# Output projection in seven block products over two query groups, and the first statistics spread by TensorE

## The chip, the cores and the metric

The kernel runs on one core of one Trainium2 chip. Its engines are TensorE (PE, matmuls into PSUM), VectorE (DVE), ScalarE (ACT), GpSimd (POOL) and SyncE (SP, which here only issues DMAs). The metric is the device time of one execution in microseconds; a profiled execution also gives the span from the first to the last event of the program.

## The reference

Input x is [2, 2048, 2048], so T = 4096 tokens of C = 2048 features; D = 512.

```
xn   = layernorm(x)                                # no scale, no shift
qkv  = xn @ Wqkv + bqkv ; q, k, v = split(qkv)     # Wqkv [2048, 1536]
attn = softmax(q @ k.T / sqrt(512)) @ v            # per batch of 2048 tokens
a    = attn @ Wo + bo                              # Wo [512, 2048]
s    = (xn @ Wq.T) @ keys.T                        # router, 64 experts
gate = softmax over the 16 largest of s, 0 elsewhere
z    = (xn @ A.T) * gate, each gate over 8 columns # A [512, 2048]
out  = x + a + 2 * (z @ B.T)                       # B.T [512, 2048]
```

## The kernel before, in words

All matmuls are made in three passes: each operand is split into a high part (a copy into the 32-bit type of TensorE, on ACT) and a low part (what is left, on DVE), and high x high, high x low and low x high are added up in one PSUM bank. Hence the names `w_hi`/`w_lo`, `r_hi`/`r_lo`, `q_hi`/`q_lo`, `p_hi`/`p_lo`, `f_hi`/`f_lo`.

**Phase A** (`phase_a`, 0 to about 1376 us) makes k, q, z and v for four groups of 1024 tokens. In each group the product of the normalised x with the weights is done as seven block products (`ORDER`, idx 0 to 6) of eight steps (s), in which two half-sized blocks of x and of the weights, or sums of them, meet. Mean and reciprocal deviation of a token are statistics over its row; they are needed as rows over all partitions (`mean_rstd`). For the first 512 tokens TensorE spreads them (a product of ones with a diagonal, L775). For the second 512 tokens of the first group, ACT (`moments`) and DVE (`stats_of_tile`) compute them in idx 0, ACT stores them to `stat_scratch` (L549) and loads them back broadcast (L555), and `normalise` of DVE waits for that (semaphore `s_mld`), in idx 1, ahead of its own next `split_weights`.

**Phase B** (`phase_b`) goes through eight query groups t of 512 queries. Its matmuls come in items: an item is one [128, 1024] block of keys, values or weights, held in a ring of four slots (`r_hi`, `r_lo`), and takes 24 matmuls. A turn is `scores(t)` (8 items), `output(t-1)` (16 items, the projection of the previous group: 8 column-and-input pieces of z and of attention per column block of 512), `values(t)` (8 items). The softmax of group t (maximum over the keys, `query_maxima`, spread of the maximum by TensorE, `less_maximum` on DVE, `exponential` on ACT, `sums` on POOL) runs beside `output(t-1)`; group 0 has no output to run beside, so `softmax_start` stands between `scores(0)` and `values(0)`. The low parts of the probabilities (`p_lo`) are made in `values`, from a ring of four.

The first time that a block is used it is split on the chip and stored to `split_scratch` (`keep`); later it is loaded in both parts (`fetch`). SP runs through its own program and waits at each load for the slot, four items ahead. The order of each engine's work is that of the Python functions of the same name: each engine works through its program in order, and a wait holds up all behind it.

In `output`, the residual rows of x are loaded into `res`, POOL adds the bias to them (L1770), DVE adds the finished PSUM bank (`take_output`, L1877), and SP stores the tile, 256 KB at a time. The attention result is taken in `take_attention` and split into `f_hi`/`f_lo`; z is transposed by TensorE.

## Time and profile before

| | |
|---|---|
| median of 3 runs | 2846.6 us (2846.41 to 2846.97) |
| profiled execution, time | 2843.56 us |
| profiled execution, span | 2841.0 us |
| PE busy | 97% of the span |
| DVE / ACT / POOL busy | 53% / 30% / 14% |
| HBM traffic | 223 GB/s over the span |

The first row is what a comparison of two kernels goes by. The profiled execution is a single one; its span is what the positions in the trace add up to. "Busy" is the time in which an engine has an instruction shown; on PE such instructions overlap each other.

### The profile page before, as it was taken

The numbers are of one execution on the slowest core, as the hardware profiler recorded it, in microseconds if no ns is written. First come the engines' busy times: TensorE is split into PE (matmuls) and PEld (weight loads), VectorE is DVE, ScalarE is ACT, GpSimd is POOL, SyncE is SP. The second block draws the span as 40 slices with busy tenths as digits, with TensorE's granted clock in tenths as the row PEclk, the third lists the DMA queues.
The fourth block names the chain that finished last, engine by engine and source line by source line (L and its number), as shares of the span: only waits on it lengthen the run. The fifth ranks groups of instructions, "written<-read, shape, count | busy, mean of one in ns | idle before, by whom it ended". The sixth has DMA issues, their size and how long they took to land.

```text
span 2841.0 us, 33300 instructions
## 1 busy us (share of the span) xinstructions
PE 2749.1 (97%) x12096; PEld 2244.6 (79%) x12096; DVE 1496.1 (53%) x1875; ACT 854.7 (30%) x1146; POOL 389.6 (14%) x293
## 2 busy tenths in 40 slices
PE   6888999999999999999979999999999999999999
PEld 4676878878888888888868788888888888888887
DVE  6665876467745776455574634324444344333431
ACT  3552225622364233322242221111322212112110
POOL 0011000000000000000031504205032050320501
PEclk9999999999999999999989999999999999999999
DMA  7589665455555364324766967758688686775866
GB/s 299 184 300 319 218 209 199 148 163 178 174 200 157 119 216 138 97 97 163 253 244 247 343 226 253 279 203 296 240 275 303 238 287 216 250 281 197 284 233 234
DMA packets 268159, 636.01 MB, mean 224 GB/s; under 512 B 30192, under 2 KB 54896, under 8 KB 263792
## 3 DMA queue, kind: packets, MB, share of 16 engines
q1 hardware_dynamic: 233968, 546.54, 56.2%
q10 hardware_dynamic: 28288, 66.62, 6.8%
q0 software_dynamic: 5760, 20.97, 2.1%
q8 instruction: 86, 1.41, 0.2%
q14 instruction: 57, 0.47, 0.1%
HBM read 499.79 MB, written 134.25 MB: 223 GB/s over the span
## 4 chain that ended last, share of the span: by engine, by line
PE 85%; DVE 5%; DMA 4%; ACT 3%; issue 2%; SPq 0%; POOL 0%; ACTq 0%; DVEq 0%; POOLq 0%
PE psum L750 35%; PE psum L1632 15%; PE psum L1634 15%; PE psum L1633 15%; PE psum L687 2%; DMA stat_scratch<-mv 2%; DMA w_raw<-t_scratch 1%; ACT rows L534 1%; DVE prob L1834 1%; DMA w_raw<-W_blocks 1%; DVE r_lo L1806 1%; ACT w_hi L479 1%; DVE w_lo L800 1%; ACT rows L537 1%; PE psum L1755 0%
## 5 line engine op out<-in xcount | busy, mean ns | idle before, releaser
L800 DVE TENSOR_TENSOR w_lo<-w_raw,w_hi 128x1024 fp32r<-128x1024 f32 x224 | 274.2, 1224 | 433.7 <-ACT w_hi L479 433.5
L479 ACT ACTIVATE w_hi<-w_raw 128x1024 fp32r<-128x1024 f32 x224 | 237.5, 1060 | 775.2 <-PE psum L750 677.8
L1632 PE MATMUL psum<-r_hi,f_hi 128*128 128x512 f32 x1024 | 401.9, 392 | 4.6 <-DVE r_lo L1806 3.3
L1634 PE MATMUL psum<-r_hi,f_lo 128*128 128x512 f32 x1024 | 399.2, 390 | 0.0
L1633 PE MATMUL psum<-r_lo,f_hi 128*128 128x512 f32 x1024 | 399.1, 390 | 0.0
L750 PE MATMUL psum<-s_hi,w_hi 128*128 128x512 f32 x896 | 353.7, 395 | 28.1 <-DVE w_lo L800 16.4
L750 PE MATMUL psum<-w_hi,s_hi 128*128 128x512 f32 x896 | 351.4, 392 | 15.9 <-DVE w_lo L800 14.9
L750 PE MATMUL psum<-s_hi,w_lo 128*128 128x512 f32 x896 | 351.3, 392 | 0.0
L750 PE MATMUL psum<-s_lo,w_hi 128*128 128x512 f32 x896 | 351.3, 392 | 0.0
L750 PE MATMUL psum<-w_lo,s_hi 128*128 128x512 f32 x896 | 350.3, 391 | 0.0
L750 PE MATMUL psum<-w_hi,s_lo 128*128 128x512 f32 x896 | 350.2, 391 | 0.0
L1770 POOL TENSOR_TENSOR res<-res,b_out 128x512 f32<-128x512 f32 x128 | 183.5, 1463 | 798.3 <-DMA res<-x 798.2
L1877 DVE TENSOR_TENSOR res<-psum,res 128x512 f32<-128x512 f32 x128 | 86.9, 691 | 366.5 <-PE psum L1634 347.5
L1632 PEld LDWEIGHTS psum<-r_hi,f_hi 128*128 128x128 f32 x1024 | 192.5, 188 | 48.7 <-DVE r_lo L1806 4.6
L750 PEld LDWEIGHTS psum<-s_hi,w_hi 128*128 128x128 f32 x896 | 169.7, 189 | 69.7 <-DVE w_lo L800 16.5
L1634 PEld LDWEIGHTS psum<-r_hi,f_lo 128*128 128x128 f32 x1024 | 192.6, 188 | 40.5
L1633 PEld LDWEIGHTS psum<-r_lo,f_hi 128*128 128x128 f32 x1024 | 192.7, 188 | 39.2
L1632 PE MATMUL psum<-p_hi,r_hi 128*128 128x512 f32 x512 | 206.8, 404 | 11.4 <-DVE p_lo L1926 6.7
L750 PEld LDWEIGHTS psum<-w_hi,s_hi 128*128 128x128 f32 x896 | 169.0, 189 | 56.4 <-DVE w_lo L800 16.2
L1632 PE MATMUL psum<-q_hi,r_hi 128*128 128x512 f32 x512 | 200.0, 391 | 2.5 <-DVE r_lo L1806 1.7
L1634 PE MATMUL psum<-p_hi,r_lo 128*128 128x512 f32 x512 | 201.5, 394 | 0.0
L1633 PE MATMUL psum<-p_lo,r_hi 128*128 128x512 f32 x512 | 201.2, 393 | 0.0
(137 smaller groups left out, 3931.5 us busy)
## 6 DMA issues: line engine op xcount, KB each, us to landing
r_hi<-split_scratch SPq DMA_DIRECT2D x208, 512.0 KB, 3.5
r_lo<-split_scratch SPq DMA_DIRECT2D x208, 512.0 KB, 4.9
w_raw<-t_scratch SPq DMA_DIRECT2D x128, 512.0 KB, 4.0
w_raw<-W_blocks SPq DMA_DIRECT2D x96, 512.0 KB, 3.9
res<-x SPq DMA_DIRECT2D x128, 256.0 KB, 6.1
out<-res SPq DMA_DIRECT2D x128, 256.0 KB, 7.2
rows<-x ACTq DMA_DIRECT2D x29, 1024.0 KB, 5.8
xb<-xT ACTq DMA_DIRECT2D x56, 512.0 KB, 6.1
```

Source lines behind the costliest of these rows:

```text
L479: nc.scalar.activation(w_hi[:, s % RAW], w_raw[:, s % RAW], ACT.Copy).then_inc(s_whi, 1)
L534: chain.link(nc.scalar.activation(tile, tile, ACT.Identity, accum_out=total[:, col]))
L537: chain.link(nc.scalar.activation(tile, tile, ACT.Square, bias=less_mean[:, col], accum_out=squares[:, col]))
L687: mm = pe.matmul(psum[0:M_R, bank, :], wq[:, block_k + k, :], t[:, k, :], start=(k == 0 and n == 0), stop=(k == HK - 1 and n == 1))
L750: mm = pe.matmul(psum[:, bank, :], stationary, moving, start=(k == 0 and n == 0 and not chained), stop=(k == HK - 1 and n == 2), skip_grou ...
L800: nc.vector.tensor_tensor(w_lo[:, s % RAW], w_raw[:, s % RAW], w_hi[:, s % RAW].bitcast(F32), ALU.subtract).then_inc(s_wlo, 1)
L1632: pe.matmul(bank, sh, mh, start=first, stop=False)
L1633: pe.matmul(bank, sh, ml, start=False, stop=False)
L1634: return pe.matmul(bank, sl, mh, start=False, stop=last)
L1770: nc.gpsimd.tensor_tensor(res[:, slot, :], res[:, slot, :], b_out[:, c * W:(c + 1) * W], ALU.add).then_inc(b_xb, 1)
L1806: nc.vector.tensor_tensor(r_lo[:, slot, :], r_raw[:, slot, :], r_hi[:, slot, :].bitcast(F32), ALU.subtract).then_inc(b_lo, 1)
L1877: nc.vector.tensor_tensor(res[:, tile % XO, :], psum[:, O_BANK[tile], :], res[:, tile % XO, :], ALU.add).then_inc(b_oev, 1)
```

## The change

**Phase B.** The projection of attention and z takes two query groups at once. With groups 2m and 2m+1 as block rows, attention and z as block columns (x11, x12 of the first, x21, x22 of the second), and the weights Wo, B_T cut in left and right column halves (b11, b12; b21, b22), the 2x2 block product is made of seven products instead of eight, for 512 columns of each half at a time; a stage `output(w)`, w = 0 to 7, has 14 items (two per product) and gives four quarters of the result (C11, C12, C21, C22). Stages now stand in this order: S0, S1, V0, V1, then S(t), O(t-2), V(t) for t = 2 to 7, then O6, O7 (S scores, V values, O output).

- POOL makes the weight sums t1 to t4 once, beside S0 to V1, and stores them (`sum_weights`).
- DVE makes the operand sums s1 to s4 (`sum_x`) and splits each item's operand (`low_x`, ACT's half is `high_x`) into the slots of `p_hi`/`p_lo` and `q_hi`/`q_lo`. Before, there was one set of `f_hi`/`f_lo` per group.
- Product 0 belongs in all four quarters: it stays in PSUM where product 2 is added on top of it, and ACT copies it out (`take_p1`); POOL adds the copy to the other three quarters (`add_p1`). DVE adds the other banks (`take_product`).
- The raw blocks of stages 0 and 1 lie in the two halves of `q_raw`. Stores and loads of rows are 1 MB each.

**Phase A.** The second 512 tokens' statistics of the first group are computed earlier, from rows that are loaded right behind the first four tiles, and spread by TensorE (`spread_own`, 8 matmuls) instead of through DRAM. DVE takes two of the four tiles (before: one). `MIX0` starts one step earlier, and for the first three steps `norm_pair` stands ahead of `split_weights`.

```
-    S_IT, O_IT, V_IT = KEYT // 2, 16, KEYT // 2
+    LEN = {"S": KEYT // 2, "V": KEYT // 2, "O": 14}
+    PRODUCTS = [("x11", "b11"), ("s3", "t3"), ("x12", "b21"), ("x22", "t4"), ("s2", "t2"), ("s4", "b22"), ("s1", "t1")]
+    CHAINED = (2, 3, 6)
+    BANK_A, BANK_B, Z_BANK = [4, 5, 2, 3], [6, 0, 1, 7], [3, 4, 5]
+    X_SUMS = {"x11": 0, "x12": 0, "x22": 0, "s1": 1, "s2": 2, "s3": 1, "s4": 3}
+    STAGES = [("S", 0), ("S", 1), ("V", 0), ("V", 1)]
+    for t in range(2, NQ):
+        STAGES += [("S", t), ("O", t - 2), ("V", t)]
+    STAGES += [("O", NQ - 2), ("O", NQ - 1)]
...
+                if kind == "O":          # fetch of a raw block, SP
+                    sp.wait_ge(b_qlo, 2 * (t + 3))
+                    if i >= 2:
+                        sp.wait_ge(b_lo, order - 2 + 1)
...
+        def sum_x(w, j):
...
+            nc.vector.tensor_tensor(low, x21, x22, ALU.add).then_inc(b_xsum, 1)
+            if steps >= 2:
+                dve.wait_ge(b_xsum, base + 1)
+                nc.vector.tensor_tensor(low, low, x11, ALU.subtract).then_inc(b_xsum, 1)
+            if steps == 3:
+                dve.wait_ge(b_xsum, base + 2)
+                nc.vector.tensor_tensor(low, x12, low, ALU.subtract).then_inc(b_xsum, 1)
...
+        def output(w):                   # DVE
+            t = w + 2
+            for i in range(LEN["O"]):
+                split_next("O", w, i)
+                if i == 0 and t < NQ:
+                    maximum(t, KEYT - 2)
+                    maximum(t, KEYT - 1)
...
+                if i >= 4 and i // 2 - 1 < NP - 1:
+                    take_product(w, i // 2 - 1, (0, 1) if i % 2 == 0 else (2, 3))
+                if i == 0 and w < NQ - 1:
+                    sum_x(w, 2)
+                if i + 2 < LEN["O"]:
+                    low_x(w, i + 2)
...
+                if i == 1 and t < NQ:
+                    query_maxima(t, MISC_S)
+                if t < NQ and 3 <= i <= 7:
+                    less_maximum(t, 2 * i - 6)
+                    less_maximum(t, 2 * i - 5)
+                if i + 3 < LEN["O"]:
+                    sum_x(w, i + 3)
...
+        def values(t):                   # DVE
+                if t >= 2 and i == 0:
+                    take_product(t - 2, NP - 1, range(QT))
...
+                if i <= 2 and t != 1:
+                    less_maximum(t, 10 + 2 * i)
+                    less_maximum(t, 11 + 2 * i)
...
+        def add_p1(w, c):                # POOL
+            for j in range(QT):
+                pool.wait_ge(b_p1, w * QT + j + 1)
...
+                nc.gpsimd.tensor_tensor(out_tile(w, c, j), out_tile(w, c, j), p1_tile(j), ALU.add
+                                        ).then_inc(b_p1add, 1)
...
+        def store(w, c):                 # SP
+            base, col = out_rows(w, c)
+            sp.wait_ge(b_oev, w * EVS + {C11: 8, C21: 16, C12: EVS, C22: EVS}[c])
...
+                    if static(g) and g == 0 and (idx, s) == (0, 6):
+                        spread_own()
+        def spread_own():                # PE
+            for a in range(2):
+                bank_read(pe, 0, 0, 0, a)
+                pe.wait_ge(s_diag, HT + 2 + a)
+                for j in range(HT):
+                    mm = pe.matmul(psum[:, a, j * P:(j + 1) * P], ones[:],
+                                   part[:, 2, HT + a, j * P:(j + 1) * P], start=True, stop=True)
```

On DVE, this is a whole output stage with its softmax before, the last one (L1877 adds a PSUM bank, L1834 subtracts the maximum, L1926 is the low part of a probability):

```order
L1825 TENSOR_REDUCE q_max<-psum 128x4
L1829 TENSOR_SCALAR diag<-ident,q_max 128x128 x4
L1877 TENSOR_TENSOR res<-psum,res 128x512 x4
L1834 TENSOR_TENSOR prob<-prob,max_all 128x512 x8
L1877 TENSOR_TENSOR res<-psum,res 128x512 x4
L1834 TENSOR_TENSOR prob<-prob,max_all 128x512 x8
L1877 TENSOR_TENSOR res<-psum,res 128x512 x4
L1926 TENSOR_TENSOR p_lo<-prob,p_hi 128x512 x2
```

And this is the middle of one after the change, from item 5 to item 8 (L2256 adds a PSUM bank, L2253 is `low_x`, L2181 the subtraction, L2240, L2243, L2246 are `sum_x`):

```order
L2256 TENSOR_TENSOR part_out<-psum,part_out 128x512 x2
L2253 TENSOR_TENSOR q_lo<-zT,q_hi 128x1024
L2181 TENSOR_TENSOR prob<-prob,max_all 128x512 x2
L2240 TENSOR_TENSOR p_sum<-attn,zT 128x1024
L2243 TENSOR_TENSOR p_sum<-p_sum,attn 128x1024
L2256 TENSOR_TENSOR part_out<-psum,part_out 128x512 x2
L2253 TENSOR_TENSOR p_lo<-p_sum,p_hi 128x1024
L2181 TENSOR_TENSOR prob<-prob,max_all 128x512 x2
L2240 TENSOR_TENSOR p_sum<-attn,zT 128x1024
L2243 TENSOR_TENSOR p_sum<-p_sum,attn 128x1024
```

The sums and low parts of 1024 columns are new in this place; before, the same engine had only adds and subtractions of 512 columns here. The same engine at the start of a values stage, after the change:

```order
L2186 TENSOR_TENSOR p_lo<-prob,p_hi 128x512 x2
L2256 TENSOR_TENSOR part_out<-psum,part_out 128x512 x8
L2181 TENSOR_TENSOR prob<-prob,max_all 128x512 x4
L2186 TENSOR_TENSOR p_lo<-prob,p_hi 128x512 x2
L2181 TENSOR_TENSOR prob<-prob,max_all 128x512 x2
L2186 TENSOR_TENSOR p_lo<-prob,p_hi 128x512 x8
```

Eight adds and four subtractions now stand between the low parts of tiles 0, 1 and those of tiles 2, 3; before, four adds stood there. POOL in a late turn, before (L1770 adds the bias, L1779 and L1782 sum up the probabilities):

```order
L1779 TENSOR_TENSOR run_sum<-prob 128x512
L1782 TENSOR_TENSOR run_sum<-run_sum,prob 128x512 x4
L1770 TENSOR_TENSOR res<-res,b_out 128x512 x4
L1782 TENSOR_TENSOR run_sum<-run_sum,prob 128x512 x6
L1770 TENSOR_TENSOR res<-res,b_out 128x512 x4
L1782 TENSOR_TENSOR run_sum<-run_sum,prob 128x512 x4
```

and after (L2051 loads rows, L2065 adds the bias, L2073 adds the shared product):

```order
L2051 DMA part_out<-x 128x4x512 x4
L2065 TENSOR_TENSOR part_out<-part_out,b_out 128x512 x16
L2073 TENSOR_TENSOR part_out<-part_out,p_part 128x512 x12
L2007 TENSOR_TENSOR run_sum<-prob 128x512
L2010 TENSOR_TENSOR run_sum<-run_sum,prob 128x512 x14
```

The bias adds moved ahead of the output stage into scores, and twelve adds per stage are new.

## Rows read from the trace of the kernel before

**Rows 1.** The page: span, and busy time, share and instructions of each engine

```profile
span 2841.0 us, 33300 instructions
PE 2749.1 (97%) x12096; PEld 2244.6 (79%) x12096; DVE 1496.1 (53%) x1875; ACT 854.7 (30%) x1146; POOL 389.6 (14%) x293
```

**Rows 2.** Waits of PE: in total us, times, longest us

```profile
PE psum L750 <- DVE w_lo L800: 31.3, 9, 13.4
PE psum L775 <- DVE score L888: 17.8, 4, 9.3
...
PE psum L1632 <- DVE p_lo L1926: 6.7, 3, 2.4
PE psum L1632 <- DVE r_lo L1806: 5.0, 4, 1.9
```

**Rows 3.** Timeline of PE: start us, us; 36 matmuls apart, then a transpose

```profile
2599.71 0.39 PE L1632 MATMUL psum<-q_hi,r_hi 128*128 128x512 f32 x1
...
2607.87 0.39 PE L1632 MATMUL psum<-q_hi,r_hi 128*128 128x512 f32 x1
...
2619.76 0.60 PE L1670 MATMUL psum<-ident,run_max 128*128 128x128 f32 x4
```

**Rows 4.** Windows of 20 us; columns as in the first line

```profile
core 0: us, PE busy (x) PEld busy (x) DVE busy (x) ACT busy (x) POOL busy (x), PEclk, DMA share, GB/s
80.00:100.00 20.00, 14.06 (x60) 10.68 (x58) 5.53 (x10) 7.77 (x11) 0.00 (x0) 0.94 0.45 112
100.00:120.00 20.00, 11.85 (x46) 9.67 (x47) 15.28 (x14) 10.54 (x16) 0.00 (x0) 0.72 0.64 230
120.00:140.00 20.00, 20.00 (x90) 15.94 (x89) 18.41 (x16) 11.89 (x17) 1.45 (x2) 1.00 0.70 234
140.00:160.00 20.00, 15.94 (x59) 12.40 (x58) 16.24 (x16) 7.39 (x10) 2.17 (x3) 0.83 0.49 165
160.00:180.00 20.00, 20.00 (x92) 16.43 (x91) 9.18 (x9) 16.65 (x25) 2.06 (x3) 1.00 1.00 359
```

**Rows 5.** Chain of work in order of time: start us, us, what

```profile
22.24 2.09 PE psum L775 x8
...
85.00 9.33 DMA stat_scratch<-mv
94.72 9.74 DMA mean_rstd<-stat_scratch
```

**Rows 6.** Windows: two of 100 us in phase B's start, then output(0)

```profile
1376.00:1476.00 100.00, 83.74 (x345) 66.80 (x344) 62.32 (x75) 37.80 (x58) 23.43 (x15) 0.91 0.76 278
1476.00:1576.00 100.00, 99.99 (x452) 82.52 (x452) 47.89 (x59) 30.42 (x46) 16.61 (x11) 1.00 0.76 273
...
1534.00:1621.00 87.00, 83.69 (x364) 67.90 (x363) 55.02 (x52) 27.71 (x37) 45.52 (x29) 0.98 0.92 334
```

**Rows 7.** Timeline of DVE, two stretches: start us, us, what, xcount

```profile
1542.75 2.35 DVE L1806 TENSOR_TENSOR r_lo<-r_raw,r_hi 128x1024 fp32r<-128x1024 f32 x2
...
1919.92 2.72 DVE L1877 TENSOR_TENSOR res<-psum,res 128x512 f32<-128x512 f32 x4 [13.76 <-PE psum L1634]
1922.56 9.30 DVE L1834 TENSOR_TENSOR prob<-prob,max_all 128x512 f32<-128x512 f32 x8
...
1944.32 1.28 DVE L1834 TENSOR_TENSOR prob<-prob,max_all 128x512 f32<-128x512 f32 x2
```

**Rows 8.** Timeline of POOL beside the second of those stretches

```profile
1924.59 1.61 POOL L1779 TENSOR_TENSOR run_sum<-prob 128x512 f32<-128x512 f32 x1 [24.82 <-ACT prob L1535]
1926.28 6.73 POOL L1782 TENSOR_TENSOR run_sum<-run_sum,prob 128x512 f32<-128x512 f32 x4
1932.97 5.03 POOL L1770 TENSOR_TENSOR res<-res,b_out 128x512 f32<-128x512 f32 x4
```

**Rows 9.** Groups by line from 1555 to 1615 us: busy us, mean ns, idle before

```profile
L1632 PE MATMUL psum<-r_hi,f_hi 128*128 128x512 f32 x80 | 32.2, 403 | 3.3 <-DVE r_lo L1806 3.3
...
L1806 DVE TENSOR_TENSOR r_lo<-r_raw,r_hi 128x1024 fp32r<-128x1024 f32 x12 | 23.3, 1950 | 22.7 <-ACT r_hi L1513 22.7
...
L1877 DVE TENSOR_TENSOR res<-psum,res 128x512 f32<-128x512 f32 x12 | 7.7, 681 | 0.6 <-PE psum L1634 0.6
```

**Rows 10.** Timeline of ACT in the first softmax

```profile
1422.70 1.05 ACT L1513 ACTIVATE r_hi<-r_raw 128x1024 fp32r<-128x1024 f32 x1
...
1429.46 1.23 ACT L1535 ACTIVATE prob<-prob 128x512 f32<-128x512 f32 x2 [0.76 <-DVE prob L1834]
```

**Rows 11.** DMA issues: xcount, KB each, median us to landing

```profile
r_hi<-split_scratch SPq DMA_DIRECT2D x208, 512.0 KB, 3.5
r_lo<-split_scratch SPq DMA_DIRECT2D x208, 512.0 KB, 4.9
...
split_scratch<-r_lo SPq DMA_DIRECT2D x48, 512.0 KB, 8.4
...
r_raw<-Wo SPq DMA_DIRECT2D x8, 512.0 KB, 7.0
```

**Rows 12.** Chain of work at the end

```profile
2837.05 0.24 PE psum L1634
...
2837.31 0.69 DVE res L1877
```

More of the change, by code:

```diff
@@ L1468, in values @@
[L1468 to L1488 removed]
+                                 ).then_inc(b_z, 16)
@@ L1495, in sync @@
             for i in range(RING):
-                fetch_keys(0, i, 0)
+                fetch("S", 0, i)
             return
-        segments(sp, scores, output, values)
-        output(NQ - 1, False)
-        store_block(NQ - 1, CB - 2)
-        store_block(NQ - 1, CB - 1)
-        for slot in range(XO):
-            sp.wait_ge(b_st[slot], 16 * NQ * CB * QT // XO)
+        stages({"S": scores, "O": output, "V": values})
+        store(NQ - 1, C21)
+        store(NQ - 1, C12)
+        store(NQ - 1, C22)
@@ L1624, in scalar @@
             if step >= IPI - RING:
-                split(0, step - IPI + RING)
+                split(step - IPI + RING)
             return
-        segments(act, scores, output, values)
-        output(NQ - 1, False)
+        stages({"S": scores, "O": output, "V": values})
     def tensor(pe):
-        def three(bank, sh, sl, mh, ml, first, last):
-            pe.matmul(bank, sh, mh, start=first, stop=False)
-            pe.matmul(bank, sh, ml, start=False, stop=False)
-            return pe.matmul(bank, sl, mh, start=False, stop=last)
@@ L1720, in values @@
-        def values(t, more):
-            if static(t) and t == 0:
-                first.bank_taken(pe, MISC)
-                transpose_maxima(t)
-                broadcast_maxima(t)
-            for i in range(V_IT):
-                vh, vl = streamed(t, S_IT + O_IT + i)
+            pe.wait_ge(b_acc, (t + 1) * MAX_STEPS)
+            if t == 0:
+                pe.wait_ge(b_mall, 2)
+            elif t == 1:
+                pe.wait_ge(b_mul, inverted(0))
+            else:
+                pe.wait_ge(b_oev, (t - 1) * EVS)
@@ L1947, in vector @@
             if step >= IPI - RING:
-                split(0, step - IPI + RING)
+                split(step - IPI + RING)
             return
-        segments(dve, scores, output, values)
-        output(NQ - 1, False)
-        take_output(NQ - 1, CB - 1)
+        stages({"S": scores, "O": output, "V": values})
+        take_product(NQ - 1, NP - 1, range(QT))
     ahead.sync = lambda sp: sync(sp, True)
```

1366 lines of the change are left out of this document (855 added, 511 removed).

## The prediction

> **What bounds the kernel now.** I began with the page. TensorE (PE) is busy 97% of a span of 2841.0 us, VectorE (DVE) 53%, ScalarE (ACT) 30%, GpSimd (POOL) 14% [rows 1]; the list of waits gives PE only a few long ones [rows 2]. So PE sets the end. Its busy time misleads, though: 37 matmuls of 128x512 start between 2599.71 and 2607.87 us, 36 steps of 0.2267 us, while each is shown 0.39 us long [rows 3], because they overlap. The Trainium skill, Perfetto Trace Analysis, section Identifying the Most-Contended Engine, says that the busy share of matmuls is no good measure, since they are pipelined; who priced a matmul at its busy 0.39 would take 150 us for what I price at 87 below. One step of the streamed operand, an "item", is 24 matmuls, so 5.44 us. Every deadline below is counted in items.
>
> Then the windows. PE loses time in two places. Around 80 to 160 us three windows hold 60, 46 and 59 matmuls where an undisturbed one holds 90, at a granted clock down to 0.72 [rows 4]; the chain of work there runs through the store and the load of the statistics (9.33 and 9.74 us) [rows 5]. And in the first two attention stages: 345 matmuls from 1376 to 1476 us, 452 in the next 100 [rows 6].
>
> **The change part by part.**
>
> (a) Matmuls. The output projection was 8 groups x 16 items; now 8 stages x 14. 16 items x 24 = 384 matmuls less, x 0.2267 = **-87.1 us**. Scores, values, transposes and totals keep their number.
>
> (b) First group's statistics. The two DMAs of 9.33 and 9.74 us leave the chain. What they cost PE: 3 x 90 - (60 + 46 + 59) = 105 matmuls = 23.8 us, clock included. In their place stand 8 products of 128x128 (eight of them took 2.09 us [rows 5]) and some DVE work that moves ahead; DVE was busy 18.4 of 20 us behind the stall [rows 4], so I leave 2.7 us of local waits: **-19 us** (-8 if loads that now start together collide, -24 at best).
>
> (c) First softmax. It lay between scores(0) and values(0) with nothing to cover it: 452 - 345 = 107 matmuls = 24.3 us. Now scores(1) covers it. But the new values(0) and values(1) begin with work that PE waits for: in values(0) DVE takes the last maxima, two subtractions, ACT two exponentials and a copy, DVE the low part: about 0.8 for the copy of the last tile, 2 x 0.64, 3 x 0.62 and 0.7 = 4.6 us by [rows 7, 10], then query_maxima stands ahead of the low parts of tiles 2 and 3 (2.3), take_maximum ahead of the high part of tile 4 (2.0); values(1) has take_attention, 4.7. With contention and clock some 17: **-7 us** (-17 to +3).
>
> (d) The old output(0) lost time as well: 364 matmuls in 87 us where 4.52 per us make 393, 29 = 6.6 us [rows 6]: **-6 us**. Its successor is (e).
>
> (e) What DVE gets to do per output stage. Durations [rows 7]: an operation of 1024 columns 1.17 (2.35 for two), of 512 from SBUF 0.64 (1.28 for two), one that adds a PSUM bank 0.68 (2.72 for four). From sum_x 14 and from low_x 12 of the long ones = 30.4; 20 adds = 13.6; 10 subtractions, 2 low parts, 2 maxima = 9.0; query_maxima 1.6. That is 54.6 us in a stage in which PE needs 14 x 5.44 = 76.2, and twice about 0.6 for transposes and broadcast [rows 3], 77.4. In stages 0 and 1 the 14 splits add 16.4: 71. So DVE alone would just keep up.
>
> It isn't alone. Eight subtractions in a row took 9.30 us where the free ones take 0.64 each: POOL's additions ran from 1924.59 on, and where the two meet they take turns, one each per 1.70 us, with POOL at 6.73/4 = 1.68 instead of 5.03/4 = 1.26 [rows 7, 8]. A meeting costs DVE about 1.1 us. The 12 long splits from 1555 to 1615 us took 1.95 on average, and there PE did wait 3.3 us for them [rows 9]. The 12 adds out of PSUM in that stretch stayed at 0.68 [rows 9]. The Trainium skill, SBUF — State Buffer, section Who interferes with whom, states this as a rule: a DVE instruction with two SBUF inputs and a GpSimd instruction that reads SBUF lock each other out, for the whole instruction. The turns agree. By the rule a meeting could cost POOL's whole 1.26 us, 26 us for 21 meetings where the rows make it 23, and the sum would be some 5 us higher over stages 0 and 1. It speaks against this change: all 26 long operations of a stage have two SBUF inputs, and so have POOL's 12 new adds.
>
> POOL's adds per output stage: 12 of the shared product, 9 of the softmax sum, 21 x 1.1 = 23 us at most. Where: ACT copies the shared product at 12.5 us into the stage (after two items and the broadcast), so POOL starts near 13. DVE's slack ends in items 5 to 8, where 4, 4, 6 and 6 us of sums and low parts stand beside adds and subtractions. By hand, in us from the stage's start, steady stage, turns of 1.70 and 2.2: low_x(5) 18, subtractions 21.3, low_x(6) 24.6, low_x(7) 31.3, both sums of item 8 39.1, low_x(8) 42.4 (PE wants it at 44.4), low_x(9) 49.3 (49.9), three sums 56.0, low_x(10) 58.4 against 55.3: PE stalls 3.1, then 0.5. So **4 us** for each of stages 3 to 5 (12); stage 2 has eight more POOL adds at its start, **9**; stage 6 has no softmax, **1**; stage 7 none. Together **+22 us** (0 if the meetings fall in DVE's idle time, 45 if all cost).
>
> In stages 0 and 1 each item starts with a split that PE wants only one item later, slack 5.44 - 1.2 = 4.2 us. From 15.9 us on, DVE has 23 long operations, 10 subtractions and 10 adds before split(10): 26.9 + 6.4 + 6.8 = 40.1, with 18 meetings 60, ends at 76; PE wants it at 55.3. **20 us**. Also q_raw holds two raw blocks, where r_raw held four: a load (7.0 us from Wo, behind it the kept parts, 8.4), ACT's copy 1.06 and the split 1.2 make 10.7 per two items, whose time is 10.9 [rows 10, 11]. No slack: 3 more. **+46 us** for both (10 at the low end, 80 at the high end).
>
> (f) Start of a values stage, t = 2 to 7. The probabilities' slots are shared with the products' operands, so only tiles 0 and 1 are split ahead; before, the low parts of tiles 2 and 3 were as well. DVE first does 8 adds (PSUM, to 3.0 us after the stage begins), 4 subtractions (5.5; POOL's sums start and cost 1), then ACT an exponential and a copy of 0.62 each [rows 10], then the low part: 8.8 against a deadline of 5.44. **3.3 us x 6 = +20 us** (12 without meetings, 30 if tile 4 is late too).
>
> (g) End. Before, after the last matmul 0.7 us of DVE and about 3 us until the span's end, with stores of 256 KB [rows 1, 12]. Now the last product adds 8 times (until +3.0) and two stores of 1 MB wait for all of them; at the 359 GB/s of the window 160:180 [rows 4] 2 MB take 6 us. **+7 us** (+3 to +10).
>
> (h) Clock. Stalls were followed by stretches at half clock (granted 0.72 to 0.94) [rows 4]. In DVE-bound stretches that costs nothing; at the starts of values stages it does: **+5 us**.
>
> Hidden: the weight sums (16 POOL operations, 16 MB of traffic) lie beside four stages without deadline until take_attention(1), 174 us; SP's stores wait for adds one or two items old, with loads four items ahead. Without that cover each late load would show with its 3.5 to 4.9 us [rows 11].
>
> Sum: -87.1 - 19 - 7 - 6 + 46 + 22 + 20 + 7 + 5 = **-19 us**. It is made against the span of 2841.0 (2843.56 as timed); the median of the runs is 2846.6, so I expect 2827.5 by the median's measure.
>
> **Rivals.** *A: the meetings cost little.* For it: 21 meetings need DVE and POOL both without gaps, and DVE has 23 us free per stage. Then (e) is 10 + 0, (f) 12, (c) -12 and (h) 1, and the sum is -87 - 19 - 12 - 6 + 10 + 12 + 7 + 1 = -94, so 2753. Against it: the rows of turns. *B: DVE is the bound in all output stages, slower than before.* One mechanism: lag that starts in items 5 to 8 isn't made up, since POOL's delayed adds then meet later operations. Stages 0, 1 at 40 each, 2 to 5 at 12: +80 + 48 instead of 46 + 22, so +41, 2887 at worst; it decides from 19 us more than forecast, or 3 us in each of six stages. *C: the two-deep raw buffer sets the pace of stages 0 and 1*, 6.4 us per item instead of 5.44 and then DVE's lag on top: +13 each: 2853 in all; for it, stores of 8.4 us in one queue with the loads; against it, the chain above closes in 10.7.
>
> **How the numbers follow.** Forecast 0.50 (its own range 2805 to 2848), A 0.27, B 0.13, C 0.10. Below 2752 lies less than half of A (0.11), above 2862 two thirds of B (0.09): that is the range. A change within 0.2% (5.7 us) can't be told from none here. Faster: 0.84 of the forecast (0.42), A 0.27, a fifth of C (0.02): 0.71; same 0.10; slower 0.19.
>
> **What would show it.** Right: 11,720 matmul records (12,096 before [rows 1], less 384, and 8 new); PE's longest waits on low_x or split lines in output stages 0 and 1; p_lo waits of 2 to 4 us at six starts of values; DVE's sums at 2.2 us mean where POOL works, 1.2 elsewhere; windows at 100 us with 88 matmuls or more. Wrong: output stages of 78 us from the first on (A), or stages of 85 and more beyond the second (B).

## The result, and the profile after

The changed kernel takes 2936.7 us (median of 4 runs, 2931.1 to 2938.5) against 2846.5 us: ratio 1.0321, 95% interval 1.0308 to 1.0334. It is slower; the forecast was 2828. The page of the changed kernel, against [rows 1]:

```profile
span 2934.3 us, 32405 instructions
PE 2708.1 (92%) x11728; PEld 2203.2 (75%) x11728; DVE 1909.9 (65%) x2155; ACT 988.9 (34%) x1293; POOL 658.6 (22%) x470
PEclk9999999999999999999979999999999999999789
```

The matmul records are 368 fewer, 8 off the 11,720 forecast, because the 8 matmuls of `spread_own` stand in the trace as 16 records. Yet the span is 93.3 us longer, so PE waits more; the granted clock dips in two places, the 21st of the 40 slices (from 1467 us) and the 38th (from 2714 us). Its waits (in all, times, longest), against [rows 2]:

```profile
PE psum L1815 <- DVE p_lo L2253: 42.3, 1, 42.3
PE psum L1815 <- DVE p_lo L2186: 30.7, 9, 5.9
PE psum L1815 <- DVE r_lo L2145: 28.9, 11, 5.5
PE psum L1815 <- issue: 26.3, 4, 14.2
PE psum L1815 <- DVE part_out L2256: 25.2, 9, 4.8
...
PE psum L1878 <- DVE diag L2176: 4.2, 1, 4.2
```

One wait of 42.3 us stands out, and the rest is spread over DVE's low parts (L2186), splits (L2145) and adds of PSUM banks (L2256). Windows that begin and end with stages (scores(0), scores(1); values(0), values(1); output 0; output 3; outputs 6, 7) show where:

```profile
core 0: us, PE busy (x) PEld busy (x) DVE busy (x) ACT busy (x) POOL busy (x), PEclk, DMA share, GB/s
1362.70:1479.40 116.70, 94.24 (x398) 76.10 (x396) 60.14 (x71) 34.95 (x56) 40.41 (x31) 0.91 0.85 314
1479.40:1601.30 121.90, 105.49 (x433) 85.50 (x434) 72.93 (x73) 44.87 (x73) 63.43 (x51) 0.88 0.74 272
1644.80:1741.10 96.30, 84.60 (x350) 68.25 (x349) 82.63 (x80) 34.42 (x42) 38.93 (x21) 0.93 0.63 223
...
2219.70:2305.30 85.60, 79.74 (x349) 65.36 (x348) 70.12 (x67) 22.89 (x30) 37.80 (x21) 0.98 0.55 200
2719.70:2923.90 204.20, 157.06 (x673) 128.69 (x672) 135.06 (x108) 33.28 (x37) 79.28 (x59) 0.88 0.51 180
```

From each stage's length I take its streamed matmuls (24 per item) times 0.2267 us; the rest I call **lost**. It includes the transposes, the total and slow-clock time. A stage ends where the next one's first matmul starts, so the wait for the start of values(0) counts in scores(1). Output 0: 96.3 - 336 x 0.2267 = 20.1; outputs 6 and 7: 204.2 - 672 x 0.2267 = 51.9. The same for every stage of both traces (us; "forecast" is the change that the prediction gives, with its terms):

| part | lost before | lost after | change | forecast |
|---|---|---|---|---|
| 384 matmuls less (a) | | | -87.1 | -87.1 |
| start and phase A (b) | 68.8 | 53.4, start 1.5 later | -13.9 | -19 |
| scores, values 0 and 1 (c) | 30.4 | 64.4 | +34.0 | -7 |
| outputs 0 and 1 (d, e) | 9.4 | 39.8 | +30.4 | +40 |
| output 2 (e) | 1.8 | 15.2 | +13.4 | +9 |
| outputs 3 to 5 (e) | 5.4 | 28.3 | +22.9 | +12 |
| outputs 6 and 7 (e) | 3.1 | 51.9 | +48.8 | +1 |
| values 2 to 7 (f, h) | 17.3 | 55.7 | +38.4 | +25 |
| end (g) | 3.7 | 10.4 | +6.7 | +7 |
| sum | | | +93.6 | -19 |

The sum agrees with the spans (+93.3). Two rows hold 89 of the 113 us by which the forecast is off: outputs 6 and 7, and the first four attention stages.

The 42.3 us in output 6, seen on POOL (first its loads of rows and bias adds for stage 6, then the stretch of the long wait) and then on DVE (start, us, what, times):

```profile
2691.67 2.99 POOL L2051 DMA_DIRECT2D part_out<-x  x4 [9.22 <-DMA out<-part_out]
2717.85 25.94 POOL L2065 TENSOR_TENSOR part_out<-part_out,b_out 128x512 f32<-128x512 f32 x16 [23.18 <-DMA part_out<-x]
...
2740.00 3.78 POOL L2065 TENSOR_TENSOR part_out<-part_out,b_out 128x512 f32<-128x512 f32 x3
2743.74 2.26 POOL L2051 DMA_DIRECT2D prob<-x  x3
2758.74 0.75 POOL L2051 DMA_DIRECT2D prob<-x  x1 [12.75 <-issue]
2759.51 14.66 POOL L2073 TENSOR_TENSOR part_out<-part_out,p_part 128x512 f32<-128x512 f32 x12
2774.13 19.52 POOL L2065 TENSOR_TENSOR prob<-prob,b_out 128x512 f32<-128x512 f32 x16
```

```profile
2760.88 0.69 DVE L2256 TENSOR_TENSOR part_out<-psum,part_out 128x512 f32<-128x512 f32 x1 [24.48 <-POOL part_out L2073]
2762.10 0.69 DVE L2256 TENSOR_TENSOR part_out<-psum,part_out 128x512 f32<-128x512 f32 x1 [0.52 <-POOL part_out L2073]
2762.71 32.04 DVE L2253 TENSOR_TENSOR p_lo<-zT,p_hi 128x1024 fp32r<-128x1024 f32 x1
```

POOL first sits 12.75 us in the fourth load of rows for stage 7, while DVE waits 24.48 us for the first shared add. Then one `low_x`, 1.2 us of work, takes 32.04 us: POOL does its 12 shared adds and 16 bias adds at a pitch of 1.22 us and ends at 2793.65, and DVE gets through 1.1 us later. No turns here, unlike in [rows 7, 8].

The end of scores(1) (DVE, then POOL):

```profile
1458.49 2.31 DVE L2145 TENSOR_TENSOR r_lo<-zT,r_hi 128x1024 fp32r<-128x1024 f32 x1 [1.65 <-ACT r_hi L1611]
1460.72 5.67 DVE L2167 TENSOR_TENSOR run_max<-run_max,part_out 128x512 f32<-128x512 f32 x2
1466.31 5.58 DVE L2181 TENSOR_TENSOR prob<-prob,max_all 128x512 f32<-128x512 f32 x2
```

```profile
1459.67 3.38 POOL L2026 TENSOR_TENSOR attn<-attn 128x1024 f32<-128x1024 f32 x1
1463.13 2.71 POOL L2028 TENSOR_TENSOR attn<-attn 128x1024 f32<-128x1024 f32 x1
```

Four operations of 0.69 us take 2.8 each beside POOL's weight sums. The longest "issue" wait, 14.2 us, is the start of values(0), just behind them: it ends at 1479.36, when DVE, late by now, has made the first low part:

```profile
1478.57 1.29 DVE L2186 TENSOR_TENSOR p_lo<-prob,p_hi 128x512 fp32r<-128x512 f32 x2 [1.21 <-ACT p_hi L1665]
```

The slow clock can be counted in the same trace. Streamed matmuls follow each other at 0.2267 us; in phase B 218 of them (26 before) come 0.43 us after the one in front without a wait between, nearly all of them where the granted clock stands at 0.5, which is 1.2 GHz, in the microseconds behind a wait of PE. At 0.2 us each they cost 44 us, against 5 before; they are spread over all rows of the table except the start and the end. One such stretch lies behind the 4.5 us wait for the split of item 9 in output 0:

```profile
1711.00:1716.00 5.00, 4.86 (x12) 0.50 0.70 228
```

### The profile page after: what moved, and what is told of

It reads as the page before. It is cut to its first block, busy times and chain, and to the rows that moved or that the text cites. A ratio compares the mean times of both kernels' runs of the same rounds, so it can differ in the third digit from the quotient of the medians.

```text
span 2934.3 us, 32405 instructions
## 1 busy us (share of the span) xinstructions
PE 2708.1 (92%) x11728; PEld 2203.2 (75%) x11728; DVE 1909.9 (65%) x2155; ACT 988.9 (34%) x1293; POOL 658.6 (22%) x470
## 4 chain that ended last, share of the span: by engine, by line
PE 68%; DVE 13%; DMA 7%; issue 6%; ACT 3%; POOL 1%; SPq 1%; ACTq 0%; DVEq 0%; POOLq 0%
PE psum L752 35%; PE psum L1815 10%; PE psum L1816 10%; PE psum L1817 10%; DVE prob L2181 3%; PE psum L687 2%; DVE part_out L2256 2%; DVE p_lo L2253 1%; DMA split_scratch<-r_lo 1%; DMA w_raw<-t_scratch 1%; DMA r_lo<-split_scratch 1%; DMA stat_scratch<-mv 1%; DMA part_out<-x 1%; DVE p_sum L2240 1%; DVE r_lo L2145 1%
## 5 line engine op out<-in xcount | busy, mean ns | idle before, releaser
L752 PE MATMUL psum<-s_hi,w_hi 128*128 128x512 f32 x896 | 352.3, 393 | 11.8 <-DVE s_lo L818 6.7
L1815 PE MATMUL psum<-p_hi,r_hi 128*128 128x512 f32 x512 | 214.3, 418 | 55.8 <-DVE p_lo L2186 30.7
L1815 PE MATMUL psum<-r_hi,p_hi 128*128 128x512 f32 x496 | 200.8, 405 | 69.9 <-DVE p_lo L2253 42.3
L2010 POOL TENSOR_TENSOR run_sum<-run_sum,prob 128x512 f32<-128x512 f32 x98 | 169.8, 1733 | 279.5 <-ACT prob L1652 269.4
L1816 PE MATMUL psum<-p_lo,r_hi 128*128 128x512 f32 x512 | 208.2, 407 | 0.0
L752 PEld LDWEIGHTS psum<-s_hi,w_hi 128*128 128x128 f32 x896 | 169.1, 189 | 51.7 <-issue 14.4
L1817 PE MATMUL psum<-p_hi,r_lo 128*128 128x512 f32 x512 | 207.8, 406 | 0.0
L1816 PE MATMUL psum<-q_lo,r_hi 128*128 128x512 f32 x512 | 201.1, 393 | 0.0
L2065 POOL TENSOR_TENSOR part_out<-part_out,b_out 128x512 f32<-128x512 f32 x112 | 167.8, 1535 | 147.9 <-DMA part_out<-x 147.9
L1817 PE MATMUL psum<-q_hi,r_lo 128*128 128x512 f32 x512 | 200.8, 392 | 0.0
L1816 PE MATMUL psum<-r_lo,p_hi 128*128 128x512 f32 x496 | 198.6, 400 | 0.0
L1817 PE MATMUL psum<-r_hi,p_lo 128*128 128x512 f32 x496 | 198.4, 400 | 0.0
## 6 DMA issues: line engine op xcount, KB each, us to landing
part_out<-x POOLq DMA_DIRECT2D x28, 1024.0 KB, 14.4
```

The lines of the kernel that those rows point to most:

```text
L752: mm = pe.matmul(psum[:, bank, :], stationary, moving, start=(k == 0 and n == 0 and not chained), stop=(k == HK - 1 and n == 2), skip_grou ...
L1815: pe.matmul(bank, sh, mh, start=start, stop=False, skip_group_check=True)
L1816: pe.matmul(bank, sh, ml, start=False, stop=False, skip_group_check=True)
L1817: return pe.matmul(bank, sl, mh, start=False, stop=stop, skip_group_check=True)
L2010: nc.gpsimd.tensor_tensor(run_sum[:], run_sum[:], prob_tile(t, k), ALU.add).then_inc(b_acc, 1)
L2065: nc.gpsimd.tensor_tensor(out_tile(w, c, j), out_tile(w, c, j), b_out[:, col:col + W], ALU.add).then_inc(b_xb, 1)
```

## Experiments

The times below are single runs unless a ratio is given; the kernel before, run beside them on the same chips, had medians of 2842.4 to 2845.9 us. The edits are against the changed kernel unless said otherwise.

**e1.** Sums of weight blocks left out.

```
-            nc.gpsimd.tensor_tensor(b12, b22, b12, ALU.subtract).then_inc(b_wsum, 1)
-            pool.wait_ge(b_wsum, 4 * kt + 1)
-            nc.gpsimd.tensor_tensor(b11, b12, b11, ALU.add).then_inc(b_wsum, 1)
...
-            pool.wait_ge(b_wsum, 4 * kt + 4)
```

> Leaves out GpSimd's 16 sums of weight blocks (the blocks are loaded and stored unsummed, so the output is not the projection's). Theory M, VectorE and GpSimd lock each other out: the sums of 1024 columns (2.4 to 3.4 us each) make VectorE late in the stages scores(0) to values(1), where TensorE loses 64 us over its matmuls; without them 25 to 30 of these stay, so 35 less, about 2901 us. Rival, the order of VectorE's and ScalarE's work at the starts of values(0) and values(1) loses the time by itself: 5 less, about 2931.

2924.1 us, 12.6 less. Scores 0, 1 lost 25.6 instead of 29.6, values 0, 1 26.1 instead of 34.8; the start of values(0) waits 5.7 us instead of 14.2. The seven other traces with the same program up to there (e2, e3, e4, e7, e11, e13, e14) lose 29.8 to 32.1 in values 0, 1, so the 34.8 is high by itself, and of the 8.7 us there some 4 to 6 are the sums'. The theory's 35 was three times too much or more. This run also repeats the long operation, after a wait of the same size:

```profile
2748.18 0.69 DVE L2249 TENSOR_TENSOR part_out<-psum,part_out 128x512 f32<-128x512 f32 x1 [24.33 <-POOL part_out L2066]
...
2750.00 32.08 DVE L2246 TENSOR_TENSOR p_lo<-zT,p_hi 128x1024 fp32r<-128x1024 f32 x1
```

**e2.** Shared adds left out.

```
-            add_p1(w, C22)
-            add_p1(w, C21)
-            add_p1(w, C12)
```

> Leaves out GpSimd's 96 adds of the shared product (the output lacks that product in three quarters); VectorE waits for the bias adds instead. Theory M: output stages 0 and 1 lose 4 us each instead of 20, stage 2 6 instead of 15, stages 3 to 5 3 each instead of 9.4, stages 6 and 7 10 instead of 52; together 100 less, about 2836. Rival, VectorE's own work is the bound of stages 0 to 2: these three keep 15 us each and the time is about 2865.

2841.0 us, 96 less. Lost: outputs 0 and 1 12.4 and 11.8, output 2 8.5, outputs 3 to 5 1.4 each, 6 and 7 8.6 together. So 90 us of the outputs' 135 hang on these 96 adds, through the meetings and through output 6. Theory M is near in the time (2836), but outputs 0 and 1 keep 12 us each where it had 4.

**e3.** Loads for stage 7 behind the shared adds.

```
-            if w == NQ - 2:
-                for c in (C22, C21, C12, C11):
-                    load_rows(NQ - 1, c)
             add_p1(w, C22)
...
             if w == NQ - 2:
+                for c in (C22, C21, C12, C11):
+                    load_rows(NQ - 1, c)
```

> In output stage 6 GpSimd issues the four row loads for stage 7 behind its 12 adds of the shared product instead of ahead of them. Theory: the 15 us between GpSimd's last bias add and its first shared add go, so VectorE's wait of 24.5 us for it falls to 9. If VectorE is then shut out for the 12 adds as before for 26, TensorE's idle of 42 us falls to about 18 and the time to 2912; if it is not shut out, to about 8 and the time to 2902. Rival, the idle of 42 us is set by the late landing of the rows for stage 6: less than 5 us change.

2895.0 us. Outputs 6 and 7 lose 11.6 instead of 51.9. DVE waits 8.74 us for the first shared add, and the same `low_x` takes 1.61:

```profile
2744.32 0.69 DVE L2255 TENSOR_TENSOR part_out<-psum,part_out 128x512 f32<-128x512 f32 x1 [8.74 <-POOL part_out L2073]
...
2746.18 1.61 DVE L2252 TENSOR_TENSOR p_lo<-zT,p_hi 128x1024 fp32r<-128x1024 f32 x1
```

That beats both values expected: 40 us hang on the place of four DMA issues.

**e4.** A wait between POOL's additions.

```
+                if w == NQ - 1:
+                    pool.wait_ge(b_xb, 4 * QT * w + BIAS_ORDER[w].index(c) * QT + j)
...
+                if w == NQ - 2:
+                    wait(pool, b_p1add, w * 3 * QT + (C22, C21, C12).index(c) * QT + j)
```

> Each of GpSimd's bias adds for stage 7 and shared adds in stage 6 also waits for the one before it to be done, as its softmax sums do; nothing is moved. Theory: VectorE was shut out for 32 us because GpSimd ran 26 additions without a wait between; with the waits both take turns and VectorE's longest instruction is under 4 us. Then TensorE's idle in stage 6 is 42 - 29 = 13 to 20 us, and the time about 2910. Rival, the shut-out has another cause than the missing waits: 32 us stay, 2937.

2906.6 us; outputs 6 and 7 lose 31.6 instead of 51.9. DVE still waits 24 us, but then it has its turns:

```profile
2751.32 0.69 DVE L2260 TENSOR_TENSOR part_out<-psum,part_out 128x512 f32<-128x512 f32 x1 [24.20 <-POOL part_out L2077]
...
2753.33 1.78 DVE L2257 TENSOR_TENSOR p_lo<-zT,p_hi 128x1024 fp32r<-128x1024 f32 x1
```

So the 42 us were two things: a late start and a shut-out. e3 shortens the first and has no shut-out either; e4 removes the shut-out alone. Waits between end it. What begins it isn't settled, and the missing waits alone do not: in e3 the 16 bias adds and 12 shared adds of stage 6 follow each other without a wait, 28 in a row, and take turns with DVE. Both shut-outs on record, here and in e1, come right behind the late fourth load, with no wait for a landing between.

**e5.** The kernel before with `phase_a` of the changed kernel, and its phase B as it was but for one semaphore less (`q_max` is counted on that of `diag`).

> The kernel before with the new first phase only: the first group's statistics are spread by TensorE, the output projection stays as it was. From the two traces (phase A 13.9 us shorter, its start included) the theory gives 2846.5 - 14 = 2832.5 us, 0.9950 of before. Rival: the time won in the first phase was only moved, since the loads and stores at the border to the attention come closer together, and less than 6 us are left at the end: 2840 or more.

2831.7 us, ratio 0.9947 (0.993 to 0.9964). Term (b) is worth 14 us (10 to 20 by the interval), and they last to the end. This half of the change, alone, is faster than the kernel before.

**e6.** e3 without any weight traffic.

```
-                load_weights(0)
-                sum_weights(0)
-                load_weights(1)
...
-                return sum_scr[int(name[1]) - 1, rows, t * W:(t + 1) * W].rearrange("(a p) w -> p a w", p=P)
+                return Wo[rows, t * W:(t + 1) * W].rearrange("(a p) w -> p a w", p=P)
```

> As e3, and leaves out the sums of weight blocks with their loads and stores altogether (the products read single blocks of the weights instead, so the output is wrong). The run without the sums alone took 8.7 us off values(0), values(1) and 4.0 off scores(0), scores(1). Theory T, the DMA traffic delays the splits of scores(0) and scores(1), where the DMA share stood at 1.0: these two stages lose 12 to 16 us instead of 29.6, and the time is about 2869. Rival, the traffic costs nothing beyond the sums: 2895 - 13 = 2882.

2873.0 us. Scores 0 and 1, as a window, against the first row of windows above:

```profile
1367.90:1465.30 97.40, 88.97 (x398) 73.14 (x396) 48.15 (x71) 35.03 (x56) 13.67 (x11) 0.99 0.79 284
```

They lose 10.3 us instead of 29.5 in e3, with a DMA share of 0.79 over 97 us instead of 0.85 over 117, and a clock of 0.99 instead of 0.91. Values 0 and 1 lose 23.8 instead of 30.1. Of the 19 us in the scores, 7.4 are the start of values(0), where PE waits 6.8 us instead of 14.2; that is the sums' part, since e1, with the traffic and without the sums, has 5.7 there. Another 7.6 are waits for splits and loads, 1.6 instead of 9.2, and about 4 are slow clock. So both hold: theory T for the splits, whose loads no longer stand beside the weight traffic, and e1's theory M for the start of values(0).

**e7.** e3 with the shared adds on DVE.

```
+            if q in (1, 3, 5):
+                c = {1: C22, 3: C21, 5: C12}[q]
+                dve.wait_ge(b_xb, 4 * QT * w + (BIAS_ORDER[w].index(c) + 1) * QT)
+                for j in tiles:
+                    dve.wait_ge(b_p1, w * QT + j + 1)
+                    nc.vector.tensor_tensor(out_tile(w, c, j), out_tile(w, c, j), p1_tile(j), ALU.add
+                                            ).then_inc(b_p1add, 1)
```

> As e3, but the 12 adds of the shared product per output stage are done by VectorE, two tiles at a time ahead of the product that follows, so that GpSimd does not run beside it then. Theory: 12 x 0.68 = 8.2 us more for VectorE and 12 x 1.1 us of meetings less; stages 0 and 1 lose 20 us each as now (12.4 without any shared add, and 8.2), stage 2 12 instead of 15, stages 3 to 5 4 each instead of 9.4: 2895 - 3 - 16 = 2876. Rival, VectorE is so full in stages 0 and 1 (79 us of work in 77) that they lose 30 each: 2895 or more.

2862.5 us, 32.5 less than e3; 29.6 of it are in the outputs, and phase B happens to start 5.4 us earlier in this run. Outputs 0 and 1 lose 15.6 each, output 2 10.8, outputs 3 to 5 3.9 to 5.5. Both values expected are beaten. The busier engine does more work and is less late.

**e8.** e3 with the probabilities' parts one item earlier (DVE's edit; ACT's `high_probability` moves likewise, and tiles 0, 1 of the first two groups are made at the end of the stage before).

```
             for i in range(LEN["V"]):
                 split_next("V", t, i)
+                if i < 7:
+                    low_probability(t, 2 * i + 2)
+                    low_probability(t, 2 * i + 3)
                 if t >= 2 and i == 0:
                     take_product(t - 2, NP - 1, range(QT))
```

> As e3, with another order on ScalarE and VectorE: the high and low parts of a values item's two probability tiles are made one item earlier, ahead of the adds of the last product, the subtractions and the exponentials that stood before them. Theory: the starts of the values stages lose time because low parts stand behind other work; values(2) to values(7) lose 18 us together instead of 54, values(0) and values(1) 22 instead of 30: 2895 - 44 = 2851. Rival, these stages wait for something else (loads, the banks that the last product's adds free): less than 10 us change.

2876.7 us, 18 less instead of 44. Values 5 and 7 fell from 9.3 and 10.6 to 6.0, value 6 from 5.7 to 0.9; values 2 and 3 kept 7.4 and 14.4 and now wait for loads (`DMA r_lo<-split_scratch`, up to 6.9 us), and values 0 and 1 kept 30.9: value 0 fell from 23.7 to 14.5, and value 1 rose from 6.4 to 16.4, 8.4 of it in one wait for a copy of the gates. Half right: the order sets the late turns, loads the early ones.

**e11, e13.** POOL's sum of probabilities written in `values` instead of `output`, in e7 and in e2.

```
-            if t < NQ:
-                sums(t, range(1, 10))
...
-                sums(t, range(10, KEYT))
+                sums(t, range(1, KEYT))
```

> As e7 (shared adds on VectorE), and GpSimd adds up the probabilities of a turn in the values stage alone; nine of the fifteen additions stood in the output stage, where each met a long operation of VectorE. Theory: without the meetings stages 0 and 1 lose 8 us each instead of 15.6, stage 2 5 instead of 10.8, stages 3 to 5 2 each instead of 4.9; the values stages give 6 back, since the sum is ready later: 2862.5 - 15 - 6 - 9 + 6 = 2839. Rival, the meetings only change place: VectorE is as late in the values stages as it was early in the output stages, 2855 or more.

> The changed kernel without the shared adds (as e2, so the output lacks that product in three quarters) and with GpSimd's sum of probabilities in the values stages: in the output stages VectorE runs alone. With the sums there and no shared adds, stages 0 and 1 lost 12.4 and 11.8 us. Theory M: four or more of these were the nine meetings (9 x 1.1 = 10 us), so 5 each now, and 2841 - 14 = 2827. Rival D, VectorE's own work stands too thick in items 6 to 10 (moving the sums did not change the 15.6 us when the shared adds were VectorE's): 10 or more each, 2838 to 2843.

2861.7 and 2842.0 us: nothing. That was my mistake, not a finding on VectorE: POOL had nothing to hold it back, so it ran through its program and made the sums when the exponentials came, as before. The splits of output 0 took 1514 ns on average in e13 and 1513 in e2. Rival D is not supported by these runs; they test nothing.

**e14.** e13 with a wait that holds POOL. e15, further down, is e9 with the same wait.

```
             else:
+                pool.wait_ge(b_used, number("O", t - 2, 10) + 1)
                 sums(t, range(1, KEYT))
```

> As e13 (no shared adds, so the output lacks that product in three quarters), and GpSimd's sum of probabilities now also waits until TensorE has used item 10 of the output stage. In e13 the sums stood later in the program but ran at the same times, since nothing held GpSimd back: VectorE's splits still took 2.3 us there. Theory M: with VectorE alone for items 0 to 10, its long operations take 1.2 us, and stages 0 and 1 lose 4 us each instead of 12, stage 2 3 less; 2842 - 19 = 2823. Rival D, VectorE's own work stands too thick in items 6 to 10: 10 or more each, 2838.

2830.6 us. Output 0 in e13, then in e14:

```profile
1641.20:1729.60 88.40, 81.62 (x349) 66.19 (x347) 75.69 (x82) 34.39 (x42) 16.57 (x9) 0.96 0.69 242
```

```profile
1645.10:1726.60 81.50, 78.47 (x349) 64.10 (x348) 71.23 (x79) 34.59 (x42) 15.40 (x9) 1.00 0.75 259
```

DVE is busy 71.2 us instead of 75.7 (3 instructions fewer lie in the shorter window, about 2 us of it), and the stage loses 5.4 instead of 12.2 (output 1: 5.3 instead of 11.8). The sums' meetings are still there, but behind item 10, where PE doesn't wait for them. M holds in the main and D, with 10 or more, falls. Something of D stays: DVE works without a gap from 1684 to 1711 us, and PE waits 1.5 and 1.4 us for the splits of items 9 and 10. In the changed kernel DVE was busy 82.6 us here and the stage lost 20.1: the meetings of the shared adds and the place of the sums' together, 11 us of DVE and 15 us of PE.

**e9, e10, e12.** e9 is e11 and e8 together, with ACT's copies of the gates ahead of the exponentials; e10 and e12 move the weight work. In scores(0), with `sum_weights(0)` at the start of scores(1):

```
+                pool.wait_ge(b_used, number("S", 0, 5) + 1)
                 load_weights(0)
```

POOL's values(1), in e10 and then in e12:

```
                 sums(1, range(8, 12))
                 sum_weights(3)
                 sums(1, range(12, KEYT))
```

```
                 sum_weights(2)
                 sums(1, range(8, 10))
                 load_weights(3)
                 sums(1, range(10, KEYT))
                 sum_weights(3)
```

> e11 and e8 together, with ScalarE's copies of the transposed gates ahead of the exponentials. e8 took 18 us off in the starts of values stages, where 8.4 us were then lost to one late copy of the gates: 2839 - 18 - 7 = 2814. Rival, both edits fill the start of the values stages (low parts, adds, subtractions beside fifteen additions of GpSimd), and the gains do not add up: 2830.

> e9, and the loads and sums of weight blocks moved: the first load waits for item 5 of scores(0), its sums stand at the start of scores(1), the others in the middle of values(0) and values(1). Theory T (DMA traffic in scores(0) and scores(1) costs 19 us) and M (sums beside the end of scores(1) make values(0) start 14 us late): 12 and 8 us come back of 65, so e9 less 20, about 2795. Rival, the traffic and the sums cost the same wherever they stand in these four stages: e9 within 5 us.

> e10 with another order on GpSimd in values(0) and values(1): no load of weight blocks stands ahead of sums of probabilities that TensorE needs, and the last weight sums come behind those. In e10 TensorE waited 24.9 us for the sum of probabilities in values(1), and scores(0), scores(1) lost 10.8 us instead of 25.3. Theory: values(0) and values(1) lose 18 us instead of 44, 2838.9 - 26 = 2813, 0.989 of before. Rival: the last weight blocks are now stored too late for the third turn, and 10 us or more of it come back: 2823 or more.

e9: 2837.9 us, above both values expected. e8's edit kept its gain (values 2 to 7 lose 37.9 instead of the 57.2 of e11); the rest of the forecast was e11's gain, which had never come. e10: 2838.9 us (0.9989, 0.998 to 0.9999), the rival's number but not its reason: scores 0, 1 lose 10.8 instead of 25.3, but PE waits in values(1) behind a POOL that waits for weights:

```profile
PE psum L1895 <- POOL run_sum L2016: 24.8, 1, 24.8
```

e12: 2832.3 us (0.9954, 0.994 to 0.9967). Scores and values 0, 1 lose 31.6 instead of 51.3, and output 0 loses 25.8 instead of 15.6, since the last weight sums are late and the bias adds of stage 0 behind them meet DVE there. The rival of e12 was right.

**e15.**

> e9 with the same wait of GpSimd for item 10 of the output stage. Theory M: here VectorE has 8.2 us of shared adds more than in e14, so stages 0 and 1 lose 9 us each instead of 15.6, stages 3 to 5 2 each instead of 4.4, and the sums still end before TensorE's total in item 5 of the values stage: 2838 - 13 - 7 = 2818. Rival: VectorE is full with 79 us of own work, so stages 0 and 1 keep 14 or more, or the late sums meet the low parts of the values stage: 2832 or more.

2806.3 us, 31.6 less than e9: outputs 0 to 5 lose 33.9 instead of 55.3, values 2 to 7 32.3 instead of 37.9. Theory M holds, with more than it asked for: outputs 0 and 1 lose 9.9 and 12.3, outputs 3 to 5 1.4 each.

**e16.** e15 with a third place for the weight work.

```
+                pool.wait_ge(b_used, number("S", 0, 3) + 1)
                 load_weights(0)
...
-                sums(0, range(1, 8))
+                sums(0, range(1, 4))
                 sum_weights(1)
+                sums(0, range(4, 8))
```

> e15 and a third place for the weight blocks: first load at item 3 of scores(0), two of the four groups of sums in scores(1), the third in values(0), the last in the middle of values(1), so that the stores end before the third turn. In e12 scores(0) to values(1) lost 31.6 us instead of the 51.3 of e9, but output stage 0 lost 10 more, because the last sums came late. Theory: the 20 us come back without the 10: e15 less 18, about 2800, 0.984 of before. Rival: the third group now stands where values(0) starts and makes it wait, e15 less 8 at most.

2806.5 us, ratio 0.9867 (0.9848 to 0.9886): no better than e15, as the rival had it: one wait of 7.3 us for a split came into scores(0) and values(0) still starts 8.4 us late. Its page:

```profile
span 2806.4 us, 32429 instructions
PE 2671.8 (95%) x11728; PEld 2180.8 (78%) x11728; DVE 1893.0 (67%) x2251; ACT 986.9 (35%) x1293; POOL 494.8 (18%) x374
```

So the change does pay once POOL is out of DVE's way: 38 us, of which e5 gives 14 to phase A and leaves some 24 of the 87 us of matmuls to phase B. The other edits (low parts earlier, gate copies, weight work) are in this number too.

## Why the prediction was wrong

**(a), (g)** right. **(b)** right in kind, 14 instead of 19; e5 shows it by itself. In the 17 traces with this phase A, phase B starts 8.7 to 17.8 us earlier than before, 12.6 on average. The windows at 100 us hold 90, 83, 68 and 92 matmuls, not 88 each.

**(c)** failed, by 41 us. The sentence that failed is "Hidden: the weight sums (16 POOL operations, 16 MB of traffic) lie beside four stages without deadline". The sums have none, but DVE beside them has: I had priced POOL's meetings in the output stages and not here, where an operation of POOL is twice as long. Without sums and traffic (e6 against e3) the four stages lose 34.1 us instead of 59.6. So the weight work costs 25 us there (22 in the time of the whole run): the sums mainly at the starts of values(0) and values(1), the traffic in the splits of scores 0 and 1, where phase A's last stores, the raw loads and the kept parts already fill the DMA engines (from 1380 to 1420 us their share is 0.99 to 1.00 even in e6). Some 5 us are scatter: the seven other traces with this program lose 59.0 to 61.3 where this one loses 64.4. The last 11 are the chain at the starts of values(0) and values(1), which I had at 17 us; in e6 these two stages still lose 23.8, and the start of values(0) 6.8 more.

**(e), outputs 0 and 1** right in mechanism, and in number partly by luck: "20 us" of DVE's lag each, measured 20.1 and 19.7. But in output 0 PE's waits are 11.7 us, for the splits of items 6 to 9 and not for that of item 10; 5 are matmuls at half clock, and 1.4 are lost in a stage without any wait (e14, outputs 3 to 5). By e14 the meetings account for 15 of the 20. The 3 us each for the two-deep raw buffer did not show, and rival C with it: where PE still waits in e14, DVE is busy with its own work without a gap and not waiting for a block. Outputs 3 to 5: the mechanism was right and only its size off, 9.5 us lost instead of about 5 (4 and the 1.4); PE waits 3.3 us in item 8 and 1.3 to 2.5 in item 10 (I had 3.1 and 0.5 for low parts there), both for adds of PSUM banks (L2256) that stand behind the sums in DVE's queue, and the rest is clock (0.83 granted from 2265 to 2275) and the 1.4. e7 and e15 take it down to 4.9 and 1.4.

**(e), output 6** failed, by 48 us: "stage 6 has no softmax, **1**". I had counted DVE's work there, but not walked through POOL's queue. Its last rows land 23.9 us after their issue; 16 bias adds follow, then four DMA issues, and only then the adds that DVE wants. And "the two take turns, one each per 1.70 us" I took for a rule, from one stretch. The Trainium skill, SBUF — State Buffer, section Who interferes with whom, promises no turns: the shared ports are an exclusive lock, the engine that issues first has them for the whole instruction (it says so of VectorE's two-port modes), and issue order decides who blocks. The trace agrees that there is a lock, but it shows no such order: the subtraction starts at 2762.71, and some 25 additions that start after it in the trace go ahead of it. e4 shows that a wait between lets DVE in; why it stayed out is open.

**(h)** was mis-sized: "**+5 us**" for the clock, and "In DVE-bound stretches that costs nothing". The matmuls at half clock cost 44 us instead of 5, of which 9 lie in outputs 0 and 1. They stand in the rows of the table with their stages. How much of them would have been hidden behind DVE's lag isn't shown; with the waits they go: e16 has 74 such matmuls, 15 us.

**(f)** was right where it was worked out: values 5 and 7 wait 3.0 us for `p_lo` L2186, forecast 3.3:

```profile
2303.50 4.88 DVE L2256 TENSOR_TENSOR part_out<-psum,part_out 128x512 f32<-128x512 f32 x8 [1.44 <-PE psum L1817]
2308.29 3.58 DVE L2181 TENSOR_TENSOR prob<-prob,max_all 128x512 f32<-128x512 f32 x4
2313.09 2.37 DVE L2186 TENSOR_TENSOR p_lo<-prob,p_hi 128x512 fp32r<-128x512 f32 x2 [1.21 <-ACT p_hi L1665]
```

Eight adds, four subtractions, then the low parts: e8, which turns the order round, takes the wait away. With the slow clock behind it, it is 4.8 us per stage over the 4.5 that values 5 and 7 lose in e15, where (f) and (h) had 4.2 together. Values 3 (14.4) and 4 (9.6) lose more: value 4 has splits again ahead of each pair, and value 3 stays open: no edit brought it under 10, and its waits for loads, 2.8 us here and 5.7 to 7.0 in e8, e9, e10 and e12, are only part of it.

**The rivals.** B came nearest by its number (2887), but not by its mechanism: outputs 0 to 5 came out 67 us longer, where it had 128. Its sign, "stages of 85 and more beyond the second", came all the same (91.4, then 85.6, 85.6 and 85.6 us), halfway between the forecast's 81.4 and B's 89.4: such a sign doesn't part the two. I had given no case to a failure in the first attention stages or in the last two.

## What to carry to other kernels

Walk through the queue of every engine that holds something another waits for, GpSimd's DMA issues too, and in the last stages as well as in a steady one. Price a GpSimd operation by what VectorE has to do beside it, wherever it stands; VectorE doing the 96 shared adds itself, 12 in each output stage, was 33 us cheaper than GpSimd doing them. To move an engine's work in time, give it something to wait for: its place in the program moves nothing if the inputs are early.

## What the runs showed of the hardware

- A two-input SBUF operation of VectorE (1.2 us alone) took 32.04 and 32.08 us beside a run of some 26 additions of GpSimd without waits at a pitch of 1.22 us (1.26 in [rows 8]), and 1.78 with waits between them. A run of 28 without waits in e3 took turns with it (1.61 to 2.31). A weaker case of it, in output 2: four diagonal products, 0.28 us each alone, in 4.24 us beside bias adds, where PE waited 4.2.

```profile
2043.15 4.24 DVE L2176 TENSOR_SCALAR diag<-ident,q_max 128x128 f32<-128x128 f32 x4
```

- Beside GpSimd's sums of 1024 columns a VectorE operation of 512 columns takes 2.8 us instead of 0.69, so a meeting there costs 2.1 us, twice that of one with 512 columns.
- The fourth of the four 1 MB loads that GpSimd issues in a row for stage 7 began 12.75 us after the issue of the third had ended, 0.67 us after the third had landed (2758.07). All 16 traces with this phase B show the same 0.67 us, whatever the idle time before it (12.5 to 20 us). The four loads for stage 6 were issued within 3 us, before any had landed; what sets the two apart isn't shown.
